# An attention kernel on one Trainium2 core: key tiles in five sets instead of eight, turned maxima and inverse sums moved to between tiles 12 and 13

## What is computed

```python
q = split(xn @ q_w.T + q_b) / sqrt(32);  k = split(xn @ k_w.T + k_b);  v = split(xn @ v_w.T + v_b)
attn = softmax(q @ k.T, axis=-1)
out = (attn @ v) @ out_w.T + out_b
```

## Time and profile before

| | us |
|---|---|
| median of three runs | 4086.81 |
| profiled execution, its own time | 4089.26 |
| its span in the trace | 4087.4 |
| PE busy | 4044.5 |
| POOL busy | 3164.7 |
| DVE busy | 3075.7 |
| ACT busy | 2367.1 |

### The profile page before, as it was taken

How to read it: one execution, slowest core, us unless ns; L and a number is a source line. 1 busy time by engine, 2 the same in 40 slices (tenths; PEclk the granted TensorE clock), 3 DMA queues, 4 the chain that set the end, 5 groups by cost and what they waited for, 6 DMA issues and landing times.

```text
span 4087.4 us, 77851 instructions
## 1 busy us (share of the span) xinstructions
PE 4044.5 (99%) x21280; PEld 2493.3 (61%) x21280; DVE 3075.7 (75%) x5122; ACT 2367.1 (58%) x4515; POOL 3164.7 (77%) x1108
## 2 busy tenths in 40 slices
PE   8999999999999999999999999999999999999999
PEld 6888888755555555555555555555555555555477
DVE  4344333788888888888888888888888888888734
ACT  2222122167677677777676777776776767676621
POOL 1222222289999999999999999999999999999920
PEclk9999999999999999999999999999999999999999
DMA  4444444568888888888888888888888888888767
GB/s 173 157 170 159 153 151 159 174 148 168 176 180 176 179 170 179 173 177 174 175 178 178 176 175 175 174 171 174 178 179 178 171 176 175 177 175 177 171 211 257
DMA packets 245348, 714.80 MB, mean 175 GB/s; under 512 B 87281, under 2 KB 88305, under 8 KB 184433
## 3 DMA queue, kind: packets, MB, share of 16 engines
q0 software_dynamic: 54288, 395.34, 49.9%
q1 hardware_dynamic: 107648, 201.88, 14.5%
q10 hardware_dynamic: 83040, 113.01, 10.2%
HBM read 178.00 MB, written 136.31 MB: 77 GB/s over the span
## 4 chain that ended last, share of the span: by engine, by line
PE 63%; DMA 11%; issue 4%; POOL 2%; ACT 1%; POOLq 0%; ACTq 0%; DVE 0%; DVEq 0%
PE sm_bank L1095 20%; PE st_bank L1122 18%; PE pv_bank L1128 18%; DMA dma_sum<-pool_sum 6%; DMA dma_sum<-probs 5%; PE sm_bank L289 3%; POOL pool_sum L827 2%; PE sm_bank L1128 2%; PE st_bank L289 1%; ACT probs L901 1%; PE sm_bank L1104 0%; PE sm_bank L1122 0%; DMA q_stack<-max_row 0%; POOL dma_sum L838 0%; ACTq L900 0%
## 5 line engine op out<-in xcount | busy, mean ns | idle before, releaser
L999 DVE TENSOR_REDUCE part_max<-sm_bank 128x1 f32<-128x512 f32 x4016 | 2448.3, 682 | 368.1 <-PE sm_bank L1095 365.9
L827 POOL TENSOR_TENSOR pool_sum<-pool_sum,probs 128x2048 f32<-128x2048 f32 x504 | 2467.6, 4896 | 20.2 <-DMA dma_sum<-probs 3.7
L901 ACT ACTIVATE probs<-st_bank 128x512 f32<-128x512 f32 x3810 | 1947.9, 616 | 575.6 <-PE st_bank L1122 557.5
L1095 PE MATMUL sm_bank<-k_stack,q_stack 96*128 96x512 f32 x4016 | 1662.0, 414 | 15.4 <-issue 13.0
L1122 PE MATMUL st_bank<-q_stack,k_stack 97*128 97x512 f32 x4064 | 1619.7, 400 | 1.5 <-DMA q_stack<-max_row 1.5
L1095 PEld LDWEIGHTS sm_bank<-k_stack,q_stack 96*128 96x128 f32 x4016 | 761.7, 190 | 589.4 <-DVE part_max L999 371.5
L1128 PE MATMUL pv_bank<-probs,v_pairs 128*32 128x512 f32 x7680 | 931.2, 598 | 0.0
L1122 PEld LDWEIGHTS st_bank<-q_stack,k_stack 97*128 97x128 f32 x4064 | 772.4, 190 | 195.8 <-ACT probs L901 25.9
L1128 PEld LDWEIGHTS pv_bank<-probs,v_pairs 128*32 128x32 f32 x7680 | 202.6, 109 | 452.2 <-ACT probs L901 255.8
L838 POOL DMA_DIRECT2D dma_sum<-probs x315 | 345.8, 1098 | 99.8 <-DMA dma_sum<-probs 46.0
L433 POOL TENSOR_TENSOR y_out<-y_out,x_in 128x512 f32<-128x512 f32 x64 | 82.8, 1293 | 370.2 <-ACT y_out L465 365.7
(11 more groups left out here) (130 smaller groups left out, 3231.2 us busy)
## 6 DMA issues: line engine op xcount, KB each, us to landing
dma_sum<-probs POOLq DMA_DIRECT2D x315, 1024.0 KB, 8.3
dma_sum<-pool_sum POOLq DMA_DIRECT2D x62, 1024.0 KB, 10.2
q_stack<-s_q_hi ACTq DMA_DIRECT2D x122, 256.0 KB, 7.5
k_stack<-s_k_hi ACTq DMA_DIRECT2D x122, 256.0 KB, 4.5
x_in<-in_x SPq DMA_DIRECT2D x16, 1024.0 KB, 7.7
s_q_hi<-qk_hi SPq DMA_DIRECT2D x16, 1024.0 KB, 4.3
s_q_lo<-qk_lo SPq DMA_DIRECT2D x16, 1024.0 KB, 6.4
s_k_hi<-qk_hi SPq DMA_DIRECT2D x16, 1024.0 KB, 4.3
```

Of the source, the lines that this page charges most:

```text
L827: nc.gpsimd.tensor_tensor(total[:], one[:], tile_at(r, kt)[:], ALU.add).then_inc(pool_added, 1)
L901: nc.scalar.activation(tile_at(r, kt)[:, q * BLK:(q + 1) * BLK], score_bank(h, kt * QB + q), ACT.Exp, scale=SCALE).then_inc(probs_ready, 1)
L999: nc.vector.tensor_reduce(part_max[:, k:k + 1], sm_bank[:, sm_place(k)], AX.X, ALU.max).then_inc(max_scores_read, 1)
L1095: nc.tensor.matmul(sm_bank[:, sm_place(k)], q_st[r][0:ROWS, q * P:(q + 1) * P], k_st[r][0:ROWS, b * BLK:(b + 1) * BLK], start=True, stop=T ...
```

## The change

The key tiles are listed in five sets, 0-2, 3-5, 6-9, 10-12 and 13-15. PE issues the scores of a set and then the uses of the whole set before it. `add_up` stays behind tile 9. The turn of the maxima moves from the start of tile 14 to the start of tile 13 (`TURN_UNIT` 4), the inversion from behind `row_max` to behind unit 3 of the next first pass (`INVERTED`), the copy of the context from behind tile 1 to behind tile 2. The empty places of the first ring move to where sets begin. The orders of POOL and SP are not touched. Of the last heads, those that run in `end_of_heads` keep their order.

```diff
--- before.py
+++ after.py
@@ -35,12 +35,15 @@
 UNITS = KT * QB
 PER_TILE = UNITS // KT
 AHEAD = 4
-TURN_UNIT = 8
+TURN_UNIT = 4
 BEGIN = 16
 SUM_UNIT = 56
-SCALED = 15
+INVERTED, SCALED = 3, 15
 ST_SKIP, ST_SLOTS = 24, 66
 CUT = 10
+TILE_SETS = [[0, 1, 2], [3, 4, 5], [6, 7, 8, 9], [10, 11, 12], [13, 14, 15]]
+SET_ENDS = [tiles[-1] + 1 for tiles in TILE_SETS]
+CUT_SET = SET_ENDS.index(CUT) + 1
 LOAD_AT = [6, 7, 9, 10, 12, 13, 15]
 
 
@@ -63,7 +66,8 @@
 LAST_CONTEXT = (BATCH - 1) * TB
 
 
-SM_TURN = [*range(TURN_UNIT), "max", *range(TURN_UNIT, SUM_UNIT), "sum", *range(SUM_UNIT, UNITS), None, None]
+SM_TURN = [*range(TURN_UNIT), "max", *range(TURN_UNIT, 28), None, *range(28, 40), None, *range(40, SUM_UNIT), "sum",
+           *range(SUM_UNIT, UNITS)]
 
 
 MAX_FROM = 10
@@ -126,7 +130,7 @@
 SPARE_BEFORE = max(u for u in range(UNITS) if st_place(u) == spare_place())
 SPARE_AFTER = min(u for u in range(UNITS) if st_place(u) == spare_place())
 
-assert ST_SKIP % (2 * PER_TILE) == 0 and ST_SLOTS % ST_BANKS == 0 and SCALED + 1 == AHEAD * PER_TILE
+assert ST_SKIP // PER_TILE in SET_ENDS and CUT in SET_ENDS and SUM_UNIT == (CUT + AHEAD) * PER_TILE and ST_SLOTS % ST_BANKS == 0 and SCALED + 1 == AHEAD * PER_TILE
 assert UNITS == 64 and len(SM_TURN) % SM_BANKS == 0 and st_slot(UNITS - 1) == ST_SLOTS - 2
 
 
@@ -941,7 +945,7 @@
                 if more:
                     for kt in range(CUT):
                         exps(following, (r + 1) % GROUP, kt)
-                        if kt == 1:
+                        if kt == TILE_SETS[0][-1]:
                             copy_pv(h, r)
                         if kt in LOAD_AT and more >= GROUP:
                             load(h + GROUP, r, LOAD_AT.index(kt))
@@ -998,6 +1002,8 @@
                     dve.wait_ge(max_scores_ready, s * UNITS + k + 1)
                     nc.vector.tensor_reduce(part_max[:, k:k + 1], sm_bank[:, sm_place(k)], AX.X,
                                             ALU.max).then_inc(max_scores_read, 1)
+                if k == INVERTED and sums_of is not None:
+                    invert(*sums_of)
                 if k == SCALED and sums_of is not None:
                     scale_in_spare(*sums_of)
 
@@ -1008,15 +1014,13 @@
                         negate(s - 1)
                     maxima(s, k, units, sums_of)
 
-            def rest(s, units=True, sums_of=None):
+            def rest(s, units=True):
                 for k in range(BEGIN, UNITS):
-                    maxima(s, k, units, sums_of)
+                    maxima(s, k, units, None)
                 if units:
                     dve.wait_ge(max_scores_read, PRIME + s * UNITS + UNITS)
                     nc.vector.tensor_reduce(row_max[:], part_max[:].rearrange("p (q b) -> p q b", b=QB), AX.X,
                                             ALU.max).then_inc(row_max_ready, 1)
-                if sums_of is not None:
-                    invert(*sums_of)
 
             dve.sem_inc(max_row_ready, 1)
             rest(1)
@@ -1043,7 +1047,7 @@
 
             def body(h, r, more, following):
                 if more >= 3:
-                    rest(following + 1, sums_of=(h, r))
+                    rest(following + 1)
                     begin(following + 2, sums_of=(h, r))
                 elif more == 2:
                     rest(following + 1)
@@ -1179,12 +1183,11 @@
                     scores(h, r, kt, q)
 
             pe.sem_inc(turned_ready, 1)
-            for p in range(CUT // 2):
-                both_scores(0, 0, 2 * p, 1, 2)
-                both_scores(0, 0, 2 * p + 1, 1, 2)
-                if p:
-                    use(0, 0, 2 * p - 2)
-                    use(0, 0, 2 * p - 1)
+            for i, tiles in enumerate(TILE_SETS[:CUT_SET]):
+                for kt in tiles:
+                    both_scores(0, 0, kt, 1, 2)
+                for kt in TILE_SETS[i - 1] if i else []:
+                    use(0, 0, kt)
 
             def end_of_heads():
 
@@ -1204,25 +1207,28 @@
                 if more == 0:
                     return
                 r1 = (r + 1) % GROUP
-                for p in range(CUT // 2, (KT if more >= 2 else END_TILE) // 2):
-                    both_scores(h, r, 2 * p, to_turn, more)
-                    both_scores(h, r, 2 * p + 1, to_turn, more)
-                    use(h, r, 2 * p - 2)
-                    use(h, r, 2 * p - 1)
+                if more >= 2:
+                    for i in range(CUT_SET, len(TILE_SETS)):
+                        for kt in TILE_SETS[i]:
+                            both_scores(h, r, kt, to_turn, more)
+                        for kt in TILE_SETS[i - 1]:
+                            use(h, r, kt)
                 if more == 1:
+                    for kt in range(CUT, END_TILE):
+                        both_scores(h, r, kt, to_turn, more)
+                    for kt in TILE_SETS[CUT_SET - 1]:
+                        use(h, r, kt)
                     end_of_heads()
                 if more >= 2:
-                    for p in range(CUT // 2):
-                        both_scores(following, r1, 2 * p, to_turn + 1, more - 1)
-                        both_scores(following, r1, 2 * p + 1, to_turn + 1, more - 1)
-                        if p == 0:
-                            use(h, r, KT - 2)
-                            use(h, r, KT - 1)
-                        else:
-                            use(following, r1, 2 * p - 2)
-                            use(following, r1, 2 * p - 1)
-                        if p == CUT // 2 - 1:
-                            add_up(h, r, more)
+                    for i, tiles in enumerate(TILE_SETS[:CUT_SET]):
+                        for kt in tiles:
+                            both_scores(following, r1, kt, to_turn + 1, more - 1)
+                        for kt in TILE_SETS[i - 1]:
+                            if i == 0:
+                                use(h, r, kt)
+                            else:
+                                use(following, r1, kt)
+                    add_up(h, r, more)
 
             def output_part(n, par, j):
                 pe.wait_ge(res_ready, PRIME + n * JT + j - JT + 1)
```

## The result

The changed kernel takes 4532.41 us (median of 4 runs, 4527.62 to 4545.70), the kernel before beside it 4086.51: a ratio of 1.1094, 95% interval 1.1068 to 1.112. The forecast was slower, 4341 us, with a range up to 4405. The way was right, the size was not: 446 us instead of 254.

What follows compares the result with a forecast made beforehand. PE and POOL with its DMAs were taken to have nearly the same pace. A round of 34.4 + 2.3 + 15.5 = 52.2 us instead of 48.13 over 62 heads adds 254 us: 4341 us, range 4235 to 4405.

Steps and rivals of the forecast that it cites:

- The views and the loop: PE and POOL at nearly the same pace; use of tile 0, join 1, merge, add_up now set the round, 52.2 us.
- The part that was to decide: Use of tile 0 coming later and add_up earlier, so PE waits for the merge in front of add_up in every head.
- 34.4 us to the use of tile 0, then join 1, merge and landing: PE from add_up through tile 0's use, 34.4 us, then POOL's part to add_up, 15.5: a round of 49.9 plus delays.
- DVE, ACT and the small steps: Ring stalls, turn, inversion, scaling, context copy and tile 12's wait; delays from add_up to tile 0 of 2.3 us.
- 1.1 of DVE's stalls: PE delayed in the longer sets by DVE's pace and small steps, terms of 0.4 + 0.5 + 0.2 us a head.
- 1.2 for tile 12: First set after add_up: tile 12's exps wait for join 2's landing to reuse tile 5's buffer, 1.2 us.
- The round without the loop: Rival that DVE sets the pace if the merge lands much sooner: 48.6 us a round, about 4117 us, chance 0.10.
- The clean saving of 0.8 us a head: Five sets instead of eight on PE, 3 x 0.27 us less a head, about 50 us in 62 heads.
- the landing and the answer of POOL: From the end of tile 0's use to add_up: join 1 after 0.1, merge after 5.14, landing 10.2, together 15.5 us.
- the clock, left out of the sum: PE idle 2.6 us before add_up, then possibly half clock; 0.5 us a head, put only into the range.
- the rival that had a chance of 0.13: PE's clock falls in every head, 62 x 0.5 us, 31 us more: 4370 us, chance 0.13.
- The price: PE's clock fall behind the wait, 1.7 us, of which 1.2 lies in tile 12's wait: 0.5 us a head.

Runs made afterwards that it cites:

- Run 1: Changed kernel without the merge, both sums multiplied by ones one after the other in add_up: 4171.6 us, ratio 1.0215.
- run 2: Kernel before with one number changed, join 1 waiting for PE's use of tile 3 instead of tile 0: 4602.2 us, ratio 1.1268.
- run 3: Kernel before with join 1 waiting for PE's use of tile 1 instead of tile 0: 4086.01 us, ratio 1.0002.
- run 8: Changed kernel with the three query-part loads behind tiles 6, 7 and 9 moved behind tiles 3, 4 and 5: 4203.4 us, ratio 1.0292.
- run 4: Changed kernel with 16 matmuls, their result overwritten, put in front of add_up's wait for the merge: 4404.8 us, ratio 1.0784.
- run 5: Changed kernel with the merge issued ahead of join 1 and add 0 of the next head in POOL's order: 4424.75 us, ratio 1.0833.
- run 6: Kernel before, with its eight sets, without the merge, both sums multiplied by ones in add_up: 4157.9 us, ratio 1.0182.

## Why the forecast was right in its direction and wrong in its size

**The views and the loop: right.** The part that was to decide did. The sum "34.4 us to the use of tile 0, then join 1, merge and landing" is the round of the changed kernel at full clock, and join 1 waits for PE in each head. Run 1 shows that the loss needs the loop, run 2 that the loop alone makes such a loss, run 3 that there was slack before.

**DVE, ACT and the small steps: right in size but for tile 12.** From add_up to the end of the use of tile 0 the sum had 34.4 + 1.1 of DVE's stalls + 1.2 for tile 12 = 36.7; at full clock 35.8 were measured, so about 1.4 of stalls. The wait of tile 12 for join 2 is missing: ACT waited for such a landing 4 times in 2900 us. Join 3, which waits for that landing, starts 17.1 us after the merge (2064.15 against 2047.02), much as the 17.41 of the rows; but add_up starts 1.7 us later behind the merge than the sum had it (11.9 against 10.2), and tile 12 with it. The round without the loop was put at 48.6, there as DVE's pace, and came out at 48.75. The clean saving of 0.8 us a head shows in no run.

**The step that failed first: the landing and the answer of POOL.** The part from the use of tile 0 to add_up was put at 0.1 + 5.14 + 10.2 = 15.5. It is 0.75 + 5.16 + 11.9 = 17.8 in the head shown and 17.5 on average between 1000 and 3700 us, with a median landing of 11.4. I carried the landing over from before as a constant. It isn't one: run 8 shows that it changes with where the loads stand, and the change moves merge and loads against each other. 35.8 + 17.5 gives the 53.3 us of run 4, in place of 36.7 + 15.5 = 52.2.

**The step that failed most: the clock, left out of the sum.** The rows showed one idle stretch of 3.2 us with the clock at half behind it, and I called 2.6 us the nearer case to that and still took none. The actual idle time is 3.7 to 5.1 us, 4.4 on average, and the clock falls behind it: 2.0 us a head, 128 us by run 4. This is the rival that had a chance of 0.13, at 4370 us. The landing that was put too short doesn't explain this: in run 5 half clock follows a wait of 2.16 us, shorter than the 2.6 that the sum gave. The price failed too. The prediction put the fall at 1.7 us and let 1.2 of it lie in the wait of tile 12, a wait that isn't there; so 0.5 us was left where 2.0 were due.

| us a head | forecast | measured |
|---|---|---|
| round before | 48.13 | 48.13 |
| five sets and moved steps, without the loop | +0.5 | +0.6 |
| what the loop adds at full clock | +3.6 | +4.6 |
| the clock | 0 (0.5 in the range) | +2.0 |
| round after | 52.2 | 55.3 |

The range failed with it, as its upper end took a landing 0.5 us later and a clock that costs 0.5 us.

## What to carry to other kernels

When work is grouped into larger portions, look first for the portion's first result: here the use of tile 0 came two key tiles later and add_up two tiles of uses earlier, and what lay between went through another engine's queue. Add up such a loop around all its queues, and treat a DMA's duration in it as something that can change with what runs beside it. A new wait on PE of the size seen here has to be priced twice, once as the wait and once at the lower clock behind it.

## What the runs showed of the hardware that was not expected

- The same accumulating DMA of 1024 KB between SBUF tiles landed in 8.2 us with the three 256 KB loads out of its way and in 11.4 with them around it (medians of run 8 and the changed kernel). The same move of the loads left it at 10.1 us against 9.2 with six sets and at 10.6 against 10.2 with eight, so it isn't a rule.
- Half clock followed idle stretches of PE of 3.7 and 4.9 us in front of add_up, and one of 2.16 us in run 5; with 0.8 to 1.3 us (the heads shown of runs 4 and 8) the mean clock of the run stayed at 0.997 or above. The Trainium skill, TensorE: Matmul & The Clock Gate, section "Part 1: The HAM clock gate", says that the throttled state is the default and activity releases it; the granted clock of 0.50 behind these waits and of 1.00 in run 4, where the wait is filled with matmuls, agrees.
- Where join 1 had waited for PE, POOL started it 0.75 us after the use of tile 0 had ended (median 0.74 in the changed kernel), where ACT's copy of the sums starts within 0.1 us of add_up's end.
- The load of the turned maxima, 8 KB, takes 4.1 us in the kernel before and 6.3 in run 6 (medians between 1000 and 3600 us), and 2.2 in the changed kernel.
